# Weaving the block builds of an edge sort between quarters of the next quad's placing steps

## The chip, the cores and the metric

The kernel runs on one core of one Trainium2 chip. The metric is the device time of one execution in microseconds (us), taken without the profiler; the median of several executions is compared. A separate execution is recorded by the hardware profiler, and all rows of traces come from such executions.

## The reference

Four graph layers run on the same graph of 12500 nodes and 412500 edges (each of 200000 random pairs in both directions, and one self loop per node). Between them stand residual additions and layer norms:

```python
edge_index = jnp.stack([src, dst])
x = _layernorm(x + _L0_gnn_ref(x, src, dst, edge_type_8, ...))      # message by edge type, segment_sum over dst, gated update
x = _layernorm(x + _L1_gnn_ref(x, edge_attr_16, We, be, bias, src, dst, 12500))  # 16x16 matrix per edge from its attributes
x = _layernorm(x + _L2_gnn_ref(x, W1, root1, b1, W2, root2, b2, edge_index, edge_type_8))  # two RGCN layers, mean by relation
x = _layernorm(x + _L3_gnn_ref(x, edge_index, W1, b1, W2, b2))      # sheaf layer, messages to src and to dst
```

The edges come sorted by dst. What all layers need is the same: rows of x gathered by src, some arithmetic per edge, and a sum over dst.

## The kernel before, in words

The kernel first sorts the edges once, and the layers after it read the sorted records and selection matrices from HBM. The change lies in this sort stage (`sort_pass`) and in a few lines of the load stage that compute its loop bounds.

**Blocks, quads, steps.** Nodes are cut into 98 blocks of 128 (by dst). Four neighbouring blocks are a quad (Q = 4, QUADS = 25; the last has two real blocks). The edges of a block are read in tiles of 128; a *step* takes five tiles (C = 5) of each of the four blocks of a quad. `quad_steps[n]` is the first step of quad n. The trace below shows 175 steps for 25 quads, so seven per quad, and one step of pads behind them.

**Placing a step.** SyncE loads the attributes of the step's 20 tiles into a ring of eight places (`load_attrs`, L576), ScalarE makes sort keys and copies the fields into the ring (`prepare`, L667, L681), VectorE turns the keys into one-hot matrices (`find`, L825), TensorE counts them (`count`, `count_late`, L730 to L746), VectorE makes from the counts the address of each record (`place`, L847 to L886, the last writes `idx`), and GpSimd issues 20 indirect DMAs that scatter 128 records each into `rec[q]` in HBM (L652). It adds one to the semaphore `scattered` when it reaches the second group of four of a step; the semaphore starts at RING - 1 = 7, so that `scattered >= i + 1`, which VectorE, ScalarE and SyncE wait for, lets them be seven steps ahead of GpSimd and no more.

**Building a block.** When the steps of a quad are scattered, each of its blocks is read back as 128 rows of 40 slots (`load_records`, L584, 420 KB) and VectorE, TensorE and ScalarE make the block's selection matrices (`build` L916 to L944, `turn` with `count_sources` on TensorE, `take_rows` on ScalarE), in one of two halves of `made`. SyncE stores them (`store`, L595 and L596, 3.2 MB). Records of quad n may be read once GpSimd has reached the second group of the first step of quad n + 1: `wait_ge(scattered, i1 + RING)`, where i1 is that step.

**The order** is written out by hand, the same on each engine, and each engine does its own list in order: all steps of quad n + 1, then the four builds of quad n, then the steps of quad n + 2. On VectorE:

```python
one_quad(0)
with dve.Fori(0, QUADS - 1) as n:
    one_quad(n + 1)
    for q in range(Q):
        build(n * Q + q, q & 1)
```

GpSimd has only its 22 turns of eight steps, and no part in the builds. Loop bounds are read from SBUF into registers (`quad_range`, L537 and L538) at each quad.

Of the kernel before, what the change touches and what calls it, by code (L numbers as in the profile page):

```python
# [18 lines left out]
ALU = mybir.AluOpType  # L19
# [21 lines left out]
SPARE = 3  # L41
FIFTH = 3277
# [34 lines left out]
def memory(nc, ctx):  # L77
# [29 lines left out]
    m.quad_tile0 = sb("quad_tile0", [1, QUADS, Q], I32)  # L107
    m.spill = sb("spill", [1, 2 * Q + 1], I32)
# [45 lines left out]
def load_and_constants(nc, m, e, a, tables, rec, spills):  # L154

    with ExitStack() as ctx:
# [23 lines left out]
        limit = sb("limit", [1, QUADS])  # L180
        sofar = [sb(f"sofar{n}", [1, QUADS + 1]) for n in range(2)]
# [16 lines left out]
        with nc.Block() as block:  # L198
# [145 lines left out]
            def _(dve):  # L344
# [69 lines left out]
                link(v.tensor_reduce(sofar[0][:, 1:QUADS + 1], need[:, :, :], AX.X, ALU.max))  # L414
# [7 lines left out]
                link(v.tensor_copy(m.quad_steps[0:1, 0:QUADS + 1], sofar[1][:, :]))  # L422
                link(v.tensor_scalar(odd[:, 1:2], m.quad_steps[0:1, QUADS:QUADS + 1], RING, None, ALU.add))
# [47 lines left out]
def sort_pass(nc, m, e, attr, rec, stream, tail):  # L471

    with ExitStack() as ctx:
# [88 lines left out]
        with nc.Block() as block:  # L562
            @block.sync
            def _(sp):
                rows = attr.rearrange("(t p) f -> p t f", p=P)

                def load_attrs(n):
                    i0, i1 = quad_range(sp, n)
                    t0 = first_tiles(sp, n)
                    with sp.Fori(i0, i1) as i:  # L570
# [27 lines left out]
                def move_blocks(n, blocks):  # L598
# [12 lines left out]
                load_attrs(0)  # L611
                with sp.Fori(0, QUADS - 1) as n:
                    load_attrs(n + 1)
                    move_blocks(n, Q)
# [8 lines left out]
                move_blocks(QUADS - 1, BLOCKS - (QUADS - 1) * Q)  # L623
# [37 lines left out]
            def _(act):  # L661
# [9 lines left out]
                def prepare(n):  # L671
                    i0, i1 = quad_range(act, n)
                    t0 = first_tiles(act, n)
                    act.wait_ge(scattered, i0 + 1)
                    if not isinstance(n, int):
                        act.wait_ge(hot_made, i0 + n)
                    make_keys(n, i0, 0, t0)
                    with act.Fori(i0, i1) as i:
# [5 lines left out]
                        make_keys(n, i + 1, local(i + 1, i0) * C, t0)  # L684

# [25 lines left out]
                prepare(0)  # L711
                with act.Fori(0, QUADS - 1) as n:
# [1749 lines left out]
```

## Time and profile before

| what | value |
|---|---|
| time, median of 3 | 15384.76 us (15326.13 to 15430.24) |
| span of the profiled execution | 18591.9 us |
| sort stage in it (first indirect DMA to the last row of the stage) | 307 to 8506 us |
| GpSimd busy in the sort stage | 3529.38 us in 3520 indirect DMAs |
| VectorE busy in the sort stage | 3770.66 us |

No other time is recorded for the profiled execution than its span, so the span stands for its own time. It is 3207 us longer than the median of the executions without a profiler. The profile's busy times and its order of events can be read as they stand, but its idle times can't all be in the time that is compared.

### The profile page before, as it was taken

The page shows a single profiled execution, that of the slowest core. Times are in us where ns is not written, and L with a number is a line of the kernel's source. Part 1 is how long each engine was busy: PE and PEld are TensorE (multiplying, and loading weights), DVE is VectorE, ACT ScalarE, POOL GpSimd, SP SyncE. Part 2 cuts the span into 40 slices and gives each one's busy share as a digit, 9 for nine tenths or more (in the row PEclk, how much of TensorE's full clock was granted, in tenths as well). Part 3 has the DMA queues.
Part 4 walks back from the last instruction along what each step waited for, and adds up shares of the span by engine and source line. Part 5 has one row for each costly group of instructions (what it writes and reads, how often), then busy time and mean ns, then how long its engine had stood idle before and what let it go on. Part 6 is the DMA issues. An engine that isn't in the chain of part 4 may idle for free. (4 is left out here: it accounts for less than half of the span.)

```text
span 18591.9 us, 463365 instructions
## 1 busy us (share of the span) xinstructions
PE 11767.0 (63%) x159683; PEld 9215.4 (50%) x159684; DVE 12455.0 (67%) x20485; ACT 7662.0 (41%) x16914; POOL 4649.6 (25%) x4771
## 2 busy tenths in 40 slices
PE   1223232232323323236988999979799699999998
PEld 0112122221212212124667888856566588888887
DVE  3345354453544535447887888878788799999998
ACT  1113122221312213124665666656566455555554
POOL 2453434435344343440001111100000111111111
PEclk8555555555555555557999999999999899999999
DMA  7112111111111211115872222268788423333222
GB/s 191 43 40 70 43 61 53 48 62 43 62 51 48 63 42 62 51 55 167 228 208 96 107 108 106 104 176 235 202 235 235 117 84 85 84 85 85 85 84 71
DMA packets 1708077, 1893.34 MB, mean 102 GB/s; under 512 B 979785, under 2 KB 1415579, under 8 KB 1682683
## 3 DMA queue, kind: packets, MB, share of 16 engines
q1 hardware_dynamic: 1588957, 1851.74, 33.4%
q0 software_dynamic: 116864, 39.75, 1.4%
q14 instruction: 148, 1.21, 0.0%
q10 hardware_dynamic: 2078, 0.15, 0.0%
q8 instruction: 30, 0.49, 0.0%
HBM read 1443.55 MB, written 447.40 MB: 102 GB/s over the span
## 5 line engine op out<-in xcount | busy, mean ns | idle before, releaser
L652 POOL DMA_INDIRECT rec<-sort_ring,sort_idx x3520 | 3529.4, 1003 | 4922.3 <-issue 4375.8
L1300 DVE TENSOR_TENSOR e_full<-e_feats,e_masks 128x3840 bf16<-128x3840 bf16 x1179 | 2524.7, 2155 | 343.2 <-ACT e_feats L1258 300.0
L699 ACT CAST sort_rows_dst<-sort_ps_rows 128x512 f16<-128x512 f32 x980 | 532.1, 587 | 5085.7 <-PE sort_ps_rows L768 2659.3
L1213 PE MATMUL e_acc<-e_full,e_sel 128*128 128x384 bf16 (+1 forms) x11760 | 2121.8, 327 | 271.0 <-DVE e_full L1300 270.9
L768 PE MATMUL sort_ps_rows<-ident_h,sort_code 128*128 128x128 f16 x7840 | 1053.3, 300 | 1627.7 <-issue 684.4
L1449 PE MATMUL e_acc<-e_outer,e_sel 128*128 128x272 f32 x7840 | 1897.1, 397 | 5.3 <-DVE e_outer L1544 5.3
L875 DVE TENSOR_TENSOR sort_over<-sort_ps_late,sort_late_base 128x20 f32<-128x20 f32 x175 | 31.1, 178 | 2727.4 <-remote 2090.6
L942 DVE TENSOR_SCALAR sort_made<-sort_rows_code,code_of 128x1664 fp8e4<-128x1664 f16 x882 | 1644.1, 1937 | 192.3 <-ACT sort_rows_code L703 133.8
L730 PE MATMUL sort_ps_count<-sort_hot,upper_b 128*128 x400 | 232.3, 581 | 2422.7 <-DVE sort_hot L825 2219.5
L1256 ACT CAST e_masks<-e_kind 128x1280 bf16<-128x1280 fp8e4 x1179 | 1482.8, 1258 | 624.9 <-DVE e_full L1300 584.0
L768 PEld LDWEIGHTS sort_ps_rows<-ident_h,sort_code 128*128 128x128 f16 x7840 | 663.2, 129 | 2009.0 <-issue 1305.3
L1449 PEld LDWEIGHTS e_acc<-e_outer,e_sel 128*128 128x128 f32 x7840 | 1459.4, 190 | 283.8 <-issue 5.6
L1213 PEld LDWEIGHTS e_acc<-e_full,e_sel 128*128 128x128 fp8e4 x11760 | 1061.2, 97 | 932.9 <-issue 299.5
L730 PEld LDWEIGHTS sort_ps_count<-sort_hot,upper_b 128*128 128x128 bf16 x400 | 49.3, 123 | 2475.5 <-issue 2475.0
L1544 DVE TENSOR_TENSOR e_outer<-e_recb,e_feats 128x2720 f32<-128x2720 f32 x393 | 1173.0, 2985 | 0.0
L1200 PEld LDWEIGHTS e_got<-own,e_hot 128*128 128x128 fp8e4 x34578 | 1037.9, 96 | 194.6 <-issue 78.5
L1200 PE MATMUL e_got<-own,e_hot 128*128 128x48 bf16 x34578 | 1063.9, 183 | 47.5 <-DMA e_hot<-stream 40.7
L2120 PE MATMUL sheaf_ps_v<-w3v,sheaf_hid 128*128 128x32 f32 x7840 | 1052.5, 279 | 0.3 <-ACT sheaf_hid L2024 0.3
L2019 ACT CAST sheaf_xt<-sheaf_ps_xt 102x512 bf16<-102x512 f32 x981 | 575.0, 586 | 1124.5 <-PE sheaf_ps_xt L2093 1107.3
L2144 PE MATMUL sheaf_by_src<-sheaf_msg,sheaf_hot_t 128*128 128x16 bf16 x33939 | 1005.2, 169 | 0.0
L933 DVE TENSOR_SCALAR sort_made<-sort_rows_dst,node 128x4992 fp8e4<-128x4992 f16 x196 | 550.1, 2848 | 676.0 <-ACT sort_rows_dst L699 468.1
L2120 PEld LDWEIGHTS sheaf_ps_v<-w3v,sheaf_hid 128*128 128x128 f32 x7840 | 969.4, 195 | 61.6 <-issue 5.1
(455 smaller groups left out, 25152.8 us busy)
## 6 DMA issues: line engine op xcount, KB each, us to landing
e_hot<-stream SPq DMA_DIRECT2D x888, 480.0 KB, 3.8
stream<-sort_made SPq DMA_DIRECT2D x98, 2568.0 KB, 7.6
e_sel<-stream SPq DMA_DIRECT2D x1176, 160.0 KB, 2.8
e_st<-stream SPq DMA_DIRECT2D x99, 1888.0 KB, 7.3
sheaf_gather<-stream SPq DMA_DIRECT2D x393, 384.0 KB, 3.1
e_hot<-stream SPq DMA_DIRECT2D x294, 448.0 KB, 3.5
tail<-sort_made SPq DMA_DIRECT2D x98, 660.0 KB, 9.3
sheaf_by_dst<-tail SPq DMA_DIRECT2D x491, 128.0 KB, 3.0
```

The source lines that it names most:

```text
L652: nc.gpsimd.indirect_dma_start(out=rec[q], out_offset=bass.IndirectOffsetOnAxis(ap=idx[:, s, q, c:c + 1], axis=0), in_=ring[:, s, q, c, :] ...
L768: last = mm(ps_rows[:, n & 1, k, :], code[:, h, what, j:j + 1].to_broadcast([P, P]), m.ident_h[:, :], start=True, stop=True)
L942: v.tensor_scalar(hot3[:, js, k, :], rows_code[:, js, :], m.code_of[:, k:k + 1], None, ALU.is_equal, saturate=False)
L1200: last = mm(got[q & 1][:, n * 3 * D:(n + 1) * 3 * D], now[:, at * P:(at + 1) * P], rows, start=k == 0, stop=k == spread - 1)
L1213: last = mm(acc[h][:, 0:cols_all], now[:, n * P:(n + 1) * P], full[q & 1][:, n, :], start=j == 0, stop=j == NT - 1)
L1256: nc.scalar.copy(masks[q & 1][:, :, :, :], kinds.unsqueeze(3).to_broadcast([P, BATCH, TYPES, D]))
L1300: v.tensor_tensor(full[q & 1][:, :, 0:cols].rearrange("p j (t k f) -> p j t k f", t=TYPES, k=3), feats[q & 1][:, :, :, :].unsqueeze(2).to_ ...
L1449: last = mm(acc[h][:, 0:cols], sel[q & 1][:, n, :], outer[q & 1][:, n, :], start=j == 0, stop=j == NT - 1)
L1544: v.tensor_tensor(outer[q & 1][:, :, :].rearrange("p j (w f) -> p j w f", f=D), recb[h][:, js, 0:AW].unsqueeze(3).to_broadcast(shape), fea ...
L2019: nc.scalar.copy(xt[k][:, :], ps_xt[0:2 * K3, :]).then_inc(xt_ready, 1)
L2120: last = mm(ps_v[:, at:at + 2 * D], hid[s & 1][:, c * P:(c + 1) * P], m.w3v[:, :], start=False, stop=True, skip_group_check=True)
L2144: last = mm(src_sums((5 * j >> 1) + r), now_t[:, c, r * P:(r + 1) * P], parts[:, p, c, 1, :], start=False, stop=False, skip_group_check=True)
```

## The change

Behind each quarter of a quad's steps each engine now does one block build, one block later than it could at the earliest (LAG = 1). The quarters are made from the quad's number of steps, s: quarter u ends at (s(u+1) + 3) >> 2, which for seven steps is two, two, two and one. The loop of quad n + 1 is: two steps, the last build of quad n - 1, two steps, the first build of quad n, two steps, the second, one step, the third. A quad is given at least four steps. SyncE loads attributes quarter by quarter, and the wait for the quad's scattered records (`landed_all`) moves from behind all seven attribute loads to behind the first two. GpSimd's program is unchanged, as is what a step and a build do.

```diff
+LAG = 1
+UNITS = Q
@@ load stage, VectorE
-                link(v.tensor_reduce(sofar[0][:, 1:QUADS + 1], need[:, :, :], AX.X, ALU.max))
+                link(v.tensor_reduce(per_quad[:, :], need[:, :, :], AX.X, ALU.max))
+                link(v.tensor_scalar(sofar[0][:, 1:QUADS + 1], per_quad[:, :], float(UNITS), None, ALU.max))
...
+                for u in range(UNITS):
+                    link(v.tensor_scalar(units[:, :, u], per_quad[:, :], float(u), float(UNITS - 1), ALU.mult, ALU.add))
+                for u in range(UNITS):
+                    link(v.tensor_scalar(units[:, :, u], units[:, :, u], UNITS.bit_length() - 1, None,
+                                         ALU.arith_shift_right))
+                    link(v.tensor_tensor(units[:, :, u], units[:, :, u], m.quad_steps[0:1, 0:QUADS], ALU.add))
@@ sort stage
+        def unit_range(eng, n, u):
+            return [eng.value_load(m.unit_steps[0:1, bass.ds(n * UNITS + k, 1)], min_val=0, max_val=1 << 20)
+                    for k in (u, u + 1)]
@@ SyncE
-                def move_blocks(n, blocks):
+                def landed_all(n):
                     _, i1 = quad_range(sp, n)
                     sp.wait_ge(scattered, i1 + RING)
                     sp.sem_inc(sp_passed, 1)
-                    load_records(n * Q, n, 0)
-                    load_records(n * Q + 1, n, 1)
-                    for q in range(blocks):
-                        store(n * Q + q, q & 1)
-                        if q + 2 < blocks:
-                            load_records(n * Q + q + 2, n, q + 2)
+
+                def one_quad(n, first):
+                    i0, _ = quad_range(sp, n)
+                    t0 = first_tiles(sp, n)
+                    for u in range(UNITS):
+                        load_attrs(i0, t0, *unit_range(sp, n, u))
+                        b = (n - 1) * Q + u
+                        if not first or u >= LAG + 1:
+                            store(b - LAG - 1, (u - LAG - 1) & 1)
+                        if u == 0:
+                            landed_all(n - 1)
+                        load_records(b, n - 1, u)
@@ ScalarE
+                def one_quad(n, first):
+                    i0, t0 = enter(n)
+                    for u in range(UNITS):
+                        prepare(n, i0, t0, *unit_range(act, n, u))
+                        if not first or u >= LAG:
+                            take_rows((n - 1) * Q + u - LAG, (u - LAG) & 1)
@@ TensorE
+                    for u in range(UNITS):
+                        steps_of(n, *unit_range(pe, n, u))
+                        if not first or u >= LAG:
+                            b = (n - 1) * Q + u - LAG
+                            turn(b, (u - LAG) & 1)
+                            count_sources(b, (u - LAG) & 1)
@@ VectorE
+                def one_quad(n, first):
+                    enter(n)
+                    for u in range(UNITS):
+                        steps_of(n, *unit_range(dve, n, u))
+                        if u == UNITS - 1:
+                            dve.sem_inc(taken, 1)
+                        if not first or u >= LAG:
+                            build((n - 1) * Q + u - LAG, (u - LAG) & 1)
@@ behind the last quad, TensorE, ScalarE and VectorE
-                for b in range((QUADS - 1) * Q, BLOCKS):
+                for b in range((QUADS - 1) * Q - LAG, BLOCKS):
```

Two places in the order of the built programs. On VectorE, in the loop over quads, the end of a build. Before, in the middle of a quad's builds (L944 ends one build, L916 begins the next):

```order
L942 TENSOR_SCALAR sort_made<-sort_rows_code,code_of 128x13x128 x3
L944 TENSOR_SCALAR sort_made<-sort_rows_code,code_of 128x128
L916 ISA
L916 COPY sort_sources<-src_hi 128x15
L917 REGISTER_ALU
L917 COPY sort_sources<-src_lo 128x15
```

The changed kernel between the end of a step's placing (L933 is the old L886), a build (L964 is the old L916) and the next quarter's loop (L557 is `unit_range`):

```order
L933 TENSOR_TENSOR sort_idx<-sort_whole,sort_over 128x20
...
L964 COPY sort_sources<-src_hi 128x15
...
L557 TENSOR_LOAD unit_steps
...
L557 TENSOR_LOAD unit_steps
...
L947 UNCONDITIONAL_BRANCH
```

So a build is now followed by two register loads from SBUF and a jump into the next loop of steps, four times per quad.

On SyncE, in the loop over quads, from the attribute loads of a step to the read of the records (L600 belongs to the wait for the scattered records). Before, the loop over seven steps ends, and both records and stores follow:

```order
L576 DMA sort_ring<-in_attr 128x5x16
L570 REGISTER_ALU
L570 COMPARE_AND_BRANCH
...
L600 REGISTER_ALU
...
L584 DMA sort_recb<-rec 128x840
...
L584 DMA sort_recb<-rec 128x840
```

The changed kernel after the first quarter, which is two steps (L612 and L613 are the store, L617 the wait, L601 the read, L593 an attribute load of the next quarter):

```order
L593 DMA sort_ring<-in_attr 128x5x16
L587 REGISTER_ALU
L587 COMPARE_AND_BRANCH
...
L612 DMA stream<-sort_made 128x10272
...
L613 DMA tail<-sort_made 128x2640
...
L617 REGISTER_ALU
...
L601 DMA sort_recb<-rec 128x840
```

The store of an earlier block now stands ahead of the wait, and the attribute loads of five of the seven steps stand behind it.

## Rows read from the trace of the kernel before

**Rows 1.** The page: span, busy times, and 40 slices of the span.

```profile
span 18591.9 us, 463365 instructions
...
PE 11767.0 (63%) x159683; PEld 9215.4 (50%) x159684; DVE 12455.0 (67%) x20485; ACT 7662.0 (41%) x16914; POOL 4649.6 (25%) x4771
...
DVE  3345354453544535447887888878788799999998
...
POOL 2453434435344343440001111100000111111111
```

**Rows 2.** Windows of the span: before the sort, the sort, behind it.

```profile
core 0: us, PE busy (x) PEld busy (x) DVE busy (x) ACT busy (x) POOL busy (x), PEclk, DMA share, GB/s
0.00:307.00 307.00, 32.44 (x170) 20.15 (x171) 131.82 (x216) 68.56 (x175) 2.88 (x20) 1.00 1.04 281
307.00:8506.00 8199.00, 2468.81 (x22352) 1719.66 (x22352) 3770.66 (x5350) 1900.21 (x4397) 3529.38 (x3520) 0.52 0.18 53
8506.00:18592.00 10086.00, 9265.73 (x137161) 7475.63 (x137161) 8552.47 (x14919) 5693.22 (x12342) 1117.34 (x1231) 0.96 0.47 136
```

**Rows 3.** One line, GpSimd's indirect DMAs: count, duration ns min/median/max, waits.

```profile
L652 POOL DMA_INDIRECT rec<-sort_ring,sort_idx x3520: 962/967/2396, 307.6 to 8454.5; - x196
...
  issue: 4375.8, 3420
  DVE sort_idx L886: 541.6, 84
  DMA rec<-sort_ring,sort_idx: 4.9, 16
```

**Rows 4.** Timeline of GpSimd, start of the sort's first two steps.

```profile
start us, us, engine line op out<-in xcount [idle before <-releaser]
307.55 1.67 POOL L652 DMA_INDIRECT rec<-sort_ring,sort_idx  x1 [303.84 <-issue]
309.53 1.00 POOL L652 DMA_INDIRECT rec<-sort_ring,sort_idx  x1 [0.30 <-issue]
...
332.44 0.97 POOL L652 DMA_INDIRECT rec<-sort_ring,sort_idx  x1 [0.30 <-issue]
338.89 1.70 POOL L652 DMA_INDIRECT rec<-sort_ring,sort_idx  x1 [5.48 <-DVE sort_idx L886]
```

**Rows 5.** Timeline of GpSimd around the builds of one quad, and its last quad's.

```profile
2038.85 0.97 POOL L652 DMA_INDIRECT rec<-sort_ring,sort_idx  x1 [0.31 <-issue]
2170.03 0.97 POOL L652 DMA_INDIRECT rec<-sort_ring,sort_idx  x1 [130.22 <-issue]
...
8109.44 0.97 POOL L652 DMA_INDIRECT rec<-sort_ring,sort_idx  x1 [129.90 <-issue]
...
8454.46 0.97 POOL L652 DMA_INDIRECT rec<-sort_ring,sort_idx  x1 [0.30 <-issue]
```

**Rows 6.** Timeline of VectorE, turn to the next quad, its first step, the second.

```profile
2154.51 0.28 DVE L944 TENSOR_SCALAR sort_made<-sort_rows_code,code_of 128x128 fp8e4<-128x128 f16 x1
2157.49 0.19 DVE L893 MEMSET sort_base<- 128x160 f32 x1 [2.71 <-issue]
...
2162.84 1.06 DVE L847 TENSOR_TENSOR sort_before<-sort_ps_count,sort_base 128x400 f32<-128x400 f32 x2 [2.58 <-PE sort_ps_count L736]
...
2169.98 1.05 DVE L847 TENSOR_TENSOR sort_before<-sort_ps_count,sort_base 128x400 f32<-128x400 f32 x2
...
2198.77 0.18 DVE L875 TENSOR_TENSOR sort_over<-sort_ps_late,sort_late_base 128x20 f32<-128x20 f32 x1 [24.28 <-remote]
```

**Rows 7.** Two lines of VectorE: the wait in each step, the turn of each quad.

```profile
L875 DVE TENSOR_TENSOR sort_over<-sort_ps_late,sort_late_base x175: 169/179/180, 305.2 to 8276.8; 128x20 f32<-128x20 f32 x175
...
  remote: 2090.6, 116
...
L893 DVE MEMSET sort_base<- x25: 192/192/192, 293.0 to 8096.8; 128x160 f32 x25
...
  issue: 66.2, 25
```

**Rows 8.** Timeline of VectorE, the first build of a quad and the next two starts.

```profile
2350.24 0.17 DVE L916 COPY sort_sources<-src_hi 128x15 bf16 x1 [0.24 <-issue]
...
2350.86 3.76 DVE L909 TENSOR_TENSOR own<-sort_sources,iota 128x1470 fp8e4<-128x1470 bf16 x2
...
2363.56 11.20 DVE L942 TENSOR_SCALAR sort_made<-sort_rows_code,code_of 128x1664 fp8e4<-128x1664 f16 x6
...
2387.50 0.18 DVE L916 COPY sort_sources<-src_hi 128x15 bf16 x1 [0.25 <-issue]
...
2417.52 0.17 DVE L916 COPY sort_sources<-src_hi 128x15 bf16 x1 [0.24 <-issue]
```

**Rows 9.** Timeline of GpSimd beside that first build.

```profile
2351.01 2.38 POOL L652 DMA_INDIRECT rec<-sort_ring,sort_idx  x1 [7.24 <-DVE sort_idx L886]
2353.69 1.76 POOL L652 DMA_INDIRECT rec<-sort_ring,sort_idx  x1 [0.30 <-issue]
2355.76 0.96 POOL L652 DMA_INDIRECT rec<-sort_ring,sort_idx  x1 [0.30 <-issue]
...
2364.65 0.96 POOL L652 DMA_INDIRECT rec<-sort_ring,sort_idx  x1 [0.30 <-issue]
...
2377.36 0.97 POOL L652 DMA_INDIRECT rec<-sort_ring,sort_idx  x1 [0.30 <-issue]
```

**Rows 10.** DMA issues by line, KB each, median us to landing.

```profile
stream<-sort_made SPq DMA_DIRECT2D x98, 2568.0 KB, 7.6
...
e_recb<-rec SPq DMA_DIRECT2D x99, 420.0 KB, 7.9
```

**Rows 11.** Timeline of SyncE's queue, the attribute loads of seven steps.

```profile
2164.98 65.78 SPq L576 DMA_DIRECT2D sort_ring<-in_attr  x28
```

More of the change, by code:

```diff
@@ L41 @@
 SPARE = 3
+LAG = 1
+UNITS = Q
+assert UNITS == 4
 FIFTH = 3277
@@ L622, in _ @@
                         sp.dma_start(ring[:, place_of(i), q, :, 0:D].squeeze(1), rows[:, 0:C, :]).then_inc(attr_in, 16)
-                move_blocks(QUADS - 1, BLOCKS - (QUADS - 1) * Q)
+                for b in range((QUADS - 1) * Q, BLOCKS):
+                    store(b - LAG - 1, (b - LAG - 1) & 1)
+                    if b == (QUADS - 1) * Q:
+                        landed_all(QUADS - 1)
+                    load_records(b, QUADS - 1, b % Q)
+                for b in range(BLOCKS - LAG - 1, BLOCKS):
+                    store(b, b & 1)
                 sp.wait_ge(spill_made, 1)
@@ L783, in _ @@
                 pe.sem_inc(ends_summed, 2)
-                one_quad(0)
-                with pe.Fori(0, QUADS - 1) as n:
-                    one_quad(n + 1)
-                    for q in range(Q):
-                        turn(n * Q + q, q & 1)
-                        count_sources(n * Q + q, q & 1)
-                for b in range((QUADS - 1) * Q, BLOCKS):
+                i0, i1 = quad_range(pe, 0)
+                count(i0)
+                steps_of(0, i0, i1)
+                one_quad(1, True)
+                with pe.Fori(1, QUADS - 1) as n:
+                    one_quad(n + 1, False)
+                for b in range((QUADS - 1) * Q - LAG, BLOCKS):
                     turn(b, b & 1)
@@ L897, in one_quad, with steps_of @@
                     find(i0, n)
-                    with dve.Fori(i0, i1) as i:
+                def steps_of(n, start, end):
+                    with dve.Fori(start, end) as i:
                         find(i + 1, n)
                         place(i, n)
-                    dve.sem_inc(taken, 1)
                 def split_sources(b, h):
@@ L948, in build, with one_quad @@
                     dve.sem_inc(built, 1)
-                one_quad(0)
-                with dve.Fori(0, QUADS - 1) as n:
-                    one_quad(n + 1)
-                    for q in range(Q):
-                        build(n * Q + q, q & 1)
+                def one_quad(n, first):
+                    enter(n)
[5 more added lines that the diff above has]
+                            build((n - 1) * Q + u - LAG, (u - LAG) & 1)
+                enter(0)
+                steps_of(0, *quad_range(dve, 0))
+                dve.sem_inc(taken, 1)
+                one_quad(1, True)
+                with dve.Fori(1, QUADS - 1) as n:
+                    one_quad(n + 1, False)
                 i0, i1 = all_steps(dve)
@@ L959, in _ @@
                         .then_inc(idx_ready, 1)
-                for b in range((QUADS - 1) * Q, BLOCKS):
+                for b in range((QUADS - 1) * Q - LAG, BLOCKS):
                     build(b, b & 1)
```

51 lines of the change are left out of this document (28 added, 23 removed).

## The prediction

> **What bounds the kernel now.** I read the page first, for the stages: the sort takes the slices in which GpSimd is busy, some 45% of the span, and no engine is over 50% busy there [rows 1]. The windows give its edges: 8199 of 18592 us, GpSimd busy 3529, VectorE 3771; behind it VectorE and TensorE are at 85% and more, and the change touches nothing [rows 2]. The whole question is the sort.
>
> There the indirect DMAs set the pace that can't be beaten. The timeline of GpSimd shows starts 1.27 us apart (0.97 busy, 0.30 between), twenty to a step, so 25.4 us a step [rows 4], and 3520 of them [rows 3], 176 steps: 4470 us. The other 3600 us of the stage GpSimd is idle in the profiled execution (8199 - 3529 - 3520 x 0.30 = 3614), most plainly once a quad: 130 us between two steps, while four builds run [rows 5]. Seven steps of 25.4 us, six waits of some 5.5 us for the next addresses [rows 4] and one of 130 us make 341, near the 8199 / 25 = 328 us of a mean quad.
>
> Read so, the weaving should give back a good part of 24 x 130 us. But the next view speaks against it. VectorE could be seven steps ahead, and it isn't: it waits in the middle of a step for a count by TensorE, 24 us in one case, until GpSimd has issued its twenty DMAs [rows 6], and that wait takes 2090.6 us in 116 steps, put down to nobody's instruction [rows 7]. A step whose counts come at once takes VectorE 7.14 us from one L847 to the next [rows 6]. Something holds the other engines while GpSimd issues in the profiled execution. And that execution is 18591.9 - 15384.8 = 3207 us longer than the median. Behind the sort there is little room for such a loss: the engines are as good as full [rows 2]. So I put all of it in the sort, where the idle time is. That is my choice, and the forecast rests on it: without the profiler the sort takes 8199 - 3207 = **4992 us**, of which GpSimd issues for at least 4470.
>
> **GpSimd's path.** Beside VectorE's instructions with two operands in SBUF an indirect DMA takes longer. The first of a step takes 1.67 or 1.70 us [rows 4], 0.7 more than the others, for 175 steps 122 us. Beside L909 of a build two took 2.38 and 1.76 [rows 9], 2.2 more together; for 98 builds at most 216 us. The rest of the same build, L933 and L942, left them at 0.96 and 0.97 [rows 8, 9]. Sum: 4470 + 122 + 216 = 4808, and 51 from the last issue at 8455.4 to 8506 [rows 2, 5]: **4859 us**, with no gap at all. The median leaves 4992 - 4859 = **133 us** of idle time for the whole sort. For one quad of seven steps GpSimd needs 7 x 26.1 + 4 x 2.2 = **191.5 us**.
>
> The Trainium skill (SBUF — State Buffer, section Who interferes with whom) says that tensor_scalar and cast can hold a port pair that GpSimd needs, and that tensor_tensor doesn't stop descriptor generation. Rows 8 and 9 show the reverse here. By that rule L933 and L942 (5.6 and 16.8 us) would stop GpSimd for 22.4 us a build, 2195 us in all, and the sort could not be under 6665 us; the median has no room for that, and the rows decide.
>
> **VectorE's path.** The turn to the next quad, from the end of L944 (2154.79) to L847 (2162.84), 8.05 us; seven steps of 7.14, 50.0; four builds of 30.0 (2387.50 to 2417.52), 120.1 [rows 6, 8]: **178.1 us** a quad, 13 under GpSimd. Does the old order let GpSimd run dry? Take as zero the moment when GpSimd reaches the second group of a quad's first step and the records of the quad before may be read. 6.75 placed steps lie ahead of it, 185 us with the two-operand stops. VectorE needs the read (7.9 us by the nearest row of 420 KB [rows 10]), 120 us of builds, the turn and one step: 143 us. It is 42 us early. So the seven places of the ring already cover the builds, and the weaving has **nothing to fill: 0 us**.
>
> **The changed order, part by part.** Steps, builds, DMAs and bytes are the same in number; 25 quads of seven steps are over the new minimum of four. Removed: nothing. Moved: at the zero of above VectorE has placed four steps instead of seven, so GpSimd has 3.75 steps, 98 us, ahead of it; VectorE owes it the read, one build, the loads of a bound and one step, 7.9 + 30 + 2.7 + 7.1 = 48 us. It is 50 us early: no loss. On SyncE the wait for the records now stands ahead of five of seven attribute loads, and a store of 3.2 MB may be queued ahead of them. Seven steps of loads took 65.8 us with their waits, so one at most 9.4 [rows 11]; with the record read (7.9) and a store (7.6 to 9.3; [rows 10] has the larger part) and a landing, taken like the read, it is 34 us. The third step is needed at 46 us. Hidden, with 12 us left; were this cover gone, GpSimd would wait for what lies beyond 46 us, once a quad.
>
> Added: on each of four engines, at each quarter, two register loads and an entry of a loop. No row shows that pair alone; the nearest is the turn of a quad on VectorE, 66.2 / 25 = 2.65 us for a back branch and two loads [rows 7], and the other end is nothing. I take the row: 4 x 2.65 = 10.6 us, and VectorE's quad becomes **188.7 us**, still 2.8 under GpSimd's. ScalarE, TensorE and SyncE pay the same and have more room: none is busier than TensorE's 2469 of 8199 [rows 2]. On the load stage some ten more VectorE instructions on 25 numbers stand in a chain. The nearest row is a VectorE instruction on 20 columns, 0.18 us [rows 7]; with as much again between two it is 4 us. At the end both orders leave the last two builds behind the last step. Sum: 0 + 4, **15389 us**. A GpSimd bound stays one, and VectorE loses most of its slack.
>
> **Rivals.** *The idle time is real and the weaving fills it.* For it: rows 5, and rows 8: a build beside a step of GpSimd took 37.3 us instead of 30.0, so 25.4 us of GpSimd were covered for 7.3. Three more such builds in 24 quads give 3 x 18.1 x 24 = 1300 us in the profiled execution, where 3614 are idle. Without the profiler only what is idle there can come back: 133 us if all of the 3207 lies in the sort. If 500 us of it lie elsewhere (the clock of TensorE is granted at 0.96 behind the sort, so not there; a longer load stage, or slower issues by GpSimd under the profiler, would do it), 633 are idle, and 1300 / 3614 of them is 228. So 15385 - 133 to - 228: about 15200 us. With the excess spread evenly, 1300 x 15385 / 18592 = 1076 us, 14300; against that stands that nothing behind the sort shows a wait like rows 7. Chance of the rival 0.24, of the large form 0.05 in it.
>
> *VectorE becomes the bound, slower.* The place is the quad loop, the price the 10.6 us of loads, less the room. It decides from 191.5 - 188.7 = 2.8 us a quad more on VectorE, or as much less on GpSimd. For it: a mean quad without the profiler is (4992 - 51) / 25 = 197.7 us, 6 more than GpSimd's path, and builds beside GpSimd need not take 30.0 (37.3 in rows 8; four of those would make 207, more than the median allows). If VectorE's path is the 197.7, nearly all of 24 x 10.6 = 254 us is added: 15385 + 254 = 15640; with a part of it, 15540. Against it: loads in a row of which a half is the branch. Chance 0.18.
> The Trainium skill (Runtime: NRT & Kernel Launch, section Instruction fetch mechanics) gives some 0.2 us for a register load and warns of a fetch stall at a taken branch outside of two pages; by its loads alone the price is 8 x 0.2 x 24 = 38 us, and no row here splits the 2.65 us.
>
> *The wait moves to SyncE.* The 12 us of cover above are gone when a store delays the attributes; 10 us a quad would be 240. It ends at the same time as the second rival and shares its chance.
>
> **How the numbers follow.** Chances: forecast 0.58, its own range 15250 to 15520; faster 0.24; slower 0.18. One per cent, 154 us, is about what a measurement of this kernel can tell from no change (the three runs span 104 us). The range reaches down to the modest form of the first rival and up to the full price of the second, **15140 to 15650**, and leaves out the large form and the tails of both, 0.15 or so.
>
> **What the profile after would show.** Right: GpSimd has no gap of 130 us any more, each build lies beside part of a step, the span of the profiled execution falls by several hundred us, up to 1300, and the median doesn't move: the profiled span and the median come apart. GpSimd's DMAs stay 1.27 us apart. The loads at a quarter cost 1 to 3 us on VectorE. The first rival is right if the median falls with the span; the second if the median rises while VectorE's gaps at the quarters are over 3 us each, or its builds beside GpSimd over 32. The forecast fails at its root if the 3207 us don't lie in the sort.

## The result, and the profile after

The changed kernel takes **15445.77 us** (median of 7 runs, 15402.72 to 15482.38), the kernel before, run beside it, 15370.91 us (7 runs, 15326.13 to 15430.24): a ratio of **1.0047 [1.0027, 1.0067]**. That is within one per cent, as forecast, but clear of 1, and 57 us above the predicted 15389. But the profiled execution of the changed kernel spans 15401.0 us where that of before spanned 18591.9 [rows 1], over 3000 us less, and the forecast had been several hundred, up to 1300.

The page of the changed kernel: span, and the 40 slices of GpSimd.

```profile
span 15401.0 us, 466034 instructions
...
POOL 1777777777777500011111100000001111111111
```

The sort now takes some 13 slices instead of 18 [rows 1], and GpSimd is at 70% and more in the twelve that lie wholly in it. This looks like the weaving at its best. It isn't: the unchanged kernel, profiled again in two of the experiments below, gave both pictures. Here is its page where its time is 15336 us (run again2):

```profile
span 15333.7 us, 463365 instructions
...
POOL 1777777777777400011111100000001111111111
```

**One fact is needed to read everything that follows: the chips used are of two kinds for this kernel.** On one (the chip of the result, and chip 2) the kernel before takes 15331 to 15371 us; on the other (chips 14 and 11) it takes 18613 to 18668 us, in every run, with the profiler or without it. They are called the fast and the slow chip here. By its span the profile before (18591.9 us) came from a slow chip, and the times beside it came from a fast one. Each set of experiments ran on one chip and is compared with the kernel before on that chip; whether it is the chip itself that differs, or something that held while a set ran, these runs don't separate.

The windows of the sort and of what follows it: the changed kernel on the fast chip; the kernel before on the fast chip; the kernel before on the slow chip. The columns are those of rows 2.

```profile
307.00:5328.00 5021.00, 2415.34 (x22352) 1705.37 (x22352) 3738.36 (x5350) 1888.30 (x4401) 3639.95 (x3520) 0.52 0.31 87
5328.00:15401.00 10073.00, 9251.30 (x137161) 7463.67 (x137161) 8552.46 (x14919) 5692.89 (x12342) 1113.06 (x1231) 0.96 0.47 136
```

```profile
307.00:5250.00 4943.00, 2398.84 (x22352) 1699.65 (x22352) 3737.80 (x5350) 1881.66 (x4399) 3676.20 (x3520) 0.54 0.30 88
5250.00:15334.00 10084.00, 9263.40 (x137161) 7480.70 (x137161) 8549.60 (x14919) 5693.75 (x12342) 1116.16 (x1231) 0.96 0.47 136
```

```profile
307.00:8505.00 8198.00, 2473.44 (x22352) 1723.30 (x22352) 3765.00 (x5351) 1899.85 (x4397) 3515.13 (x3520) 0.53 0.18 53
```

Behind the sort the stage is the same (10073, 10084, and 10086 in rows 2). The sort of the kernel before is 8198 us on the slow chip and 4943 on the fast one. The change makes it 5021: **78 us longer**. (These two profiles are of two fast chips, that of the result and chip 2. The changed kernel's own profile on chip 2 is read below.) The busy times don't tell why, since GpSimd's even falls by 36 us (3676.20 to 3639.95; 307 of its DMAs take over 1.2 us instead of 330). What GpSimd waited for does. The indirect DMAs' line, of the changed kernel and then of the kernel before, both on the fast chip (engine, operation, count, ns; then idle us and how often, by what ended it):

```profile
L681 POOL DMA_INDIRECT rec<-sort_ring,sort_idx x3520: 962/967/2957, 307.0 to 5277.7; - x196
...
  issue: 1105.2, 3346
  ACT sort_ring L713: 303.3, 1
  DMA rec<-sort_ring,sort_idx: 222.3, 159
  DMA sort_ring<-in_attr: 4.3, 14
```

```profile
L652 POOL DMA_INDIRECT rec<-sort_ring,sort_idx x3520: 962/969/2449, 307.9 to 5198.6; - x196
...
  issue: 1405.8, 3374
  DMA rec<-sort_ring,sort_idx: 108.7, 129
  DMA sort_ring<-in_attr: 4.3, 14
```

The one long wait for the load stage (some 303 us) is in "issue" before and a row of its own after, so the issue gaps are the same, 1102 and 1105 us. No address is waited for (no row for sort_idx), before or after. Attributes cost 4.3 us in both. What doubled is GpSimd's wait for its own DMAs to land, **108.7 to 222.3 us**: +113.6, less the 36.3 of busy time, is 77, against 80 by which the line's first start to its last end grew (4891.7 to 4971.7). The changed kernel profiled on chip 2 itself (run woven, 15410.9 us) shows the same at a smaller size. Its row:

```profile
  DMA rec<-sort_ring,sort_idx: 211.4, 154
```

That is +102.7, less 36.1 of busy time, 67, against 64 (4891.7 to 4955.3). Of the 77 us between the two profiled spans on this chip (15410.9 and 15333.7) some 62 lie in the sort. So two profiles of one kernel differ by 11 to 16 us here, and the terms below are no finer than that.

Where are these waits? SyncE's queue of the changed kernel on the fast chip, and GpSimd a few us later:

```profile
2086.61 0.37 SPq L612 DMA_DIRECT2D stream<-sort_made  x1
2087.16 0.36 SPq L613 DMA_DIRECT2D tail<-sort_made  x1
...
2092.04 12.27 SPq L593 DMA_DIRECT2D sort_ring<-in_attr  x8
```

```profile
2094.77 0.97 POOL L681 DMA_INDIRECT rec<-sort_ring,sort_idx  x1 [0.30 <-issue]
2099.44 0.97 POOL L681 DMA_INDIRECT rec<-sort_ring,sort_idx  x1 [3.70 <-DMA rec<-sort_ring,sort_idx]
```

A block's store (2.6 + 0.66 MB) is issued at 2086.6, and 12.8 us later GpSimd, which starts a group of four DMAs only when the group before the last has landed, waits 3.70 us. This holds throughout: of the changed kernel's waits of this kind, 86 are over 0.8 us (200.1 us together), and **after all 86 GpSimd's DMA starts 7.1 to 14.0 us behind a store's issue**. Of the kernel before it is all 62 (88.3 us together, 7.0 to 12.7 us behind a store), and of the changed kernel on chip 2 all 89 (191.1 us, 8.8 to 14.7). By chance it would be one in five: 167 and 187 of the 880 group starts lie 4 to 16 us behind a store. So the waits belong to the stores by their place. The change has more of them and longer ones, 2.3 us instead of 1.4. Some 90 of the 98 stores lie beside GpSimd's issues: 62 waits follow before, 86 and 89 after. A second DMA lies beside many stores, the read of a block's records 1.3 us behind. It is there at 42 of the 90 stores before and at 64 in woven, and the landing waits behind these are longer (1.28 and 2.25 us a store in the mean, against 0.72 and 1.90 behind the others). A part of the weaving's share may be the read's.

### The profile page after: what moved, and what is told of

Read it like the earlier page. It is cut to its first block and busy times, and to the rows that moved or that the text cites. A ratio compares the mean times of both kernels' runs of the same rounds, so it can differ in the third digit from the quotient of the medians.

```text
span 15401.0 us, 466034 instructions
## 1 busy us (share of the span) xinstructions
PE 11698.7 (76%) x159683; PEld 9188.8 (60%) x159684; DVE 12425.3 (81%) x20500; ACT 7649.1 (50%) x16914; POOL 4755.9 (31%) x4771
## 5 line engine op out<-in xcount | busy, mean ns | idle before, releaser
L681 POOL DMA_INDIRECT rec<-sort_ring,sort_idx x3520 | 3640.0, 1034 | 1635.0 <-issue 1105.2
L2202 PEld LDWEIGHTS sheaf_by_src<-sheaf_msg,sheaf_hot_t 128*128 128x128 bf16 x33939 | 969.5, 96 | 2.9 <-issue 2.9
L2082 ACT ACTIVATE sheaf_hid<-sheaf_ps_h,b 128x512 f32<-128x512 f32 x981 | 674.2, 687 | 513.4 <-PE sheaf_ps_h L2160 511.7
```

The lines of the kernel that those rows point to most:

```text
L681: nc.gpsimd.indirect_dma_start(out=rec[q], out_offset=bass.IndirectOffsetOnAxis(ap=idx[:, s, q, c:c + 1], axis=0), in_=ring[:, s, q, c, :] ...
L2082: nc.scalar.activation(hid[k][:, :], ps_h[:, :], ACT.Relu, bias=m.b1[:, 0:1]).then_inc(hid_ready, 1)
L2202: last = mm(src_sums((5 * j >> 1) + r), now_t[:, c, r * P:(r + 1) * P], parts[:, p, c, 1, :], start=False, stop=False, skip_group_check=True)
```

## The experiments

Three sets, each on one chip. The medians, and the ratio to the kernel before on that chip, with its 95% interval (it is not the ratio of the medians, and differs from it by up to 0.001). The kernel before takes 18620.6 us on chip 14, 15331.6 on chip 2 and 18667.7 on chip 11:

| kernel | chip | us | ratio |
|---|---|---|---|
| before, again (again) | 14, slow | 18613.1 | 0.999 [0.9975, 1.0005] |
| split_only | 14, slow | 18663.1 | 1.0023 [1.0009, 1.0036] |
| after_land4 | 14, slow | 18184.0 | 0.9767 [0.9741, 0.9792] |
| before_land4 | 14, slow | 18490.4 | 0.993 [0.9911, 0.9949] |
| before, again (again2) | 2, fast | 15336.3 | 1.0002 [0.999, 1.0015] |
| the changed kernel (woven) | 2, fast | 15426.4 | 1.0053 [1.0036, 1.0071] |
| split_only2 | 2, fast | 15361.2 | 1.001 [0.9999, 1.0021] |
| woven_loads | 2, fast | 15699.9 | 1.0235 [1.0211, 1.0258] |
| the changed kernel (woven2) | 11, slow | 18254.3 | 0.9779 [0.9753, 0.9806] |
| after_land4b | 11, slow | 18305.7 | 0.9809 [0.9787, 0.9832] |
| before_land4b | 11, slow | 18610.3 | 0.9978 [0.9961, 0.9995] |
| store_twice | 11, slow | 18809.1 | 1.0088 [1.0059, 1.0117] |

### First set (chip 14)

**The kernel before, once more**, without an edit.

> The kernel before, unchanged, timed against itself. Its time should be that of before (ratio 1.000 within 0.2%), which shows what the measurement can tell. Its profile decides between two readings of the 3207 us by which the profiled execution of before was longer than the median: if the order of steps and builds makes the profiler hold the engines, the new profile has a span of some 18600 us again and a gap of 130 us on GpSimd at each quad; if it was that one execution, the span is within 100 us of 15370 and GpSimd issues without gaps. The profile after had a span of 15401 us with seven steps of the first quad in a row, as before, so I expect the second.

It took 18613.1 us in the median of its timed runs, and 18651.2 profiled. The expectation was wrong: its span is long again, and so are its times. The profiler isn't what makes it long. So the choice on which the forecast rests (3207 us of profiler in the sort) fell with this run. The count by TensorE on which VectorE waits in each step is here as in rows 7 (line of VectorE, and what ended its idle time):

```profile
L875 DVE TENSOR_TENSOR sort_over<-sort_ps_late,sort_late_base x175: 170/179/180, 305.0 to 8272.5; 128x20 f32<-128x20 f32 x175
its engine sat idle before it (us, times) until:
  remote: 2631.7, 143
```

**The split loops in the old order.** The loops of the changed kernel, with its bounds, its register loads and its four loops a quad, but the builds behind the whole quad again. One engine's part of the edit; SyncE, ScalarE and TensorE have the like:

```diff
-                        if u == UNITS - 1:
-                            dve.sem_inc(taken, 1)
-                        if not first or u >= LAG:
-                            build((n - 1) * Q + u - LAG, (u - LAG) & 1)
+                    dve.sem_inc(taken, 1)
+                    for q in range(Q):
+                        build((n - 1) * Q + q, q & 1)
```

> The kernel before, with each quad's steps cut into the four loops of the change on every engine (register loads and loop entries added), but with all four builds behind them and SyncE's loads, waits and stores in the old order. Theory 'register loads': the added loads and loop entries are what costs the 75 us, so this kernel takes some 15445 us too (ratio 1.005). Theory 'collisions on GpSimd's path': the loads hide behind GpSimd, ratio 1.000 within 0.002, and the 75 us come from where the builds, stores and attribute loads now fall. In its profile VectorE still waits for records once a quad under the second theory.

18663.1, +0.23% on this chip. The gaps of a quad are as before (24, of 126.4 us in the mean against 126.8 in again); the trace puts them to another releaser, a row of its L679:

```profile
  DMA sort_ring<-in_attr: 2672.8, 22
```

The 22 waits "for attributes" are 121 us each. Attributes aren't what was late: the queue that loads them stands behind the records' wait in the old order too, and the old kernel shows the same gaps with the releaser "issue" [rows 5]. It is the name of whatever came last by the profile.

**Four semaphores instead of two** for the landing of GpSimd's DMAs, so that a group waits for the fourth before it instead of the second; in the changed kernel and in the kernel before. The edit has two more parts: GpSimd adds to `scattered` at the fourth group of a step instead of the second, so that ring places come free and records may be read two groups later, and the spare rows (`trash`, `none`) get five places instead of three. The line for the wait:

```diff
-                            pool.wait_ge(landed[at & 1], u * (16 * Q * C // 2) + (at >> 1) * (16 * Q))
+                            pool.wait_ge(landed[at & 3], u * (16 * Q * C // 4) + (at >> 2) * (16 * Q))
```

> The changed kernel, with four semaphores for the landing of GpSimd's scatters in place of two, so that a group of four waits for the group four before it and not two before it (trash rows get five places in place of three, and the place is given free at the fourth group of a step). In the profile after GpSimd waited 222 us for its own scatters to land, 159 times. Theory 'GpSimd bound': those waits go and the time falls by 100 to 220 us, to about 15230 to 15340. Theory 'VectorE bound': nothing falls, 15445 within 20 us.

> The kernel before with the same four landing semaphores. If the 75 us that the change costs are landing waits (stores and attribute loads now lying beside more of the scatters), this kernel gains less than the changed one does, and the two come out equal, within 0.2%. If the 75 us are something else, both gain the same and stay 75 us apart. With GpSimd as the bound the gain is 50 to 220 us, with VectorE none.

Ratios 0.9767 and 0.993. The kernel before gained 130 us from it, though GpSimd hardly waits for landings on this chip (7.0 us in 23, in the run of the kernel before). The repeat on chip 11 gave 57 us. The traces show where it came from: GpSimd's 24 long gaps are 117.4 us in the mean instead of 126.8, and VectorE's first build of a quad, part of which lies beside GpSimd's issues, takes 35.7 us instead of 58.4 (the third and fourth take 30.2 in both). So it is the build, and not the landing wait, that got shorter. Which part of the edit does it was not tried; the later `scattered`, which lets the builds start later, is one that could. On its own the first ratio couldn't say whether the weaving or the semaphores made the gain, and the third set had to.

### Second set (chip 2)

> The changed kernel, unchanged, beside the kernel before on one chip. The last four runs were on a chip on which the kernel before takes 18620 us, not 15371, and in all its runs, not only when profiled. So the forecast's root ('the 3207 us are the profiler's') is wrong: there are two kinds of chip for this kernel. If this is the slow kind, GpSimd has 3500 us of gaps there and each build should cover a part of a step: I expect the ratio at 0.965 to 0.985 (with four landing semaphores the changed order was 306 us faster than the old). If it is the fast kind: ratio 1.003 to 1.006, as first measured.

> The kernel before, unchanged, for a profile on this chip. On a chip of the fast kind it should have no gap of 130 us on GpSimd, GpSimd's landing waits and stops should sum to some 75 us less than the 222 + 239 us of the changed kernel's profile if collisions are the cost, and the same if the loads are. On the slow kind it is a second profile like the first.

> Steps cut into four loops on every engine, builds and SyncE's order as before. On the slow chip it cost 42 us (1.0023). Theory 'register loads': the cost of the change on the fast kind is this part, ratio 1.004 to 1.006. Theory 'collisions': 1.000 within 0.002 on the fast kind. On a slow chip again 1.002.

**woven_loads** is the changed kernel with three more pairs of register loads at each quarter, on VectorE alone:

```diff
+                        for _ in range(3):
+                            unit_range(dve, n, u)
```

> The changed kernel with three more pairs of the register loads at each quarter, on VectorE alone; their values aren't used. Twelve pairs a quad of 0.6 us each without a branch (two TENSOR_LOAD of 0.3) up to 1.9 us make 7 to 23 us on VectorE's path of a quad. If GpSimd is the bound (fast kind), VectorE waits 15 us a quad for records in the profile after and takes it out of that: under 40 us more than the changed kernel. If VectorE is the bound: 170 to 550 us more.

This chip is a fast one, and its runs settle most. The changed kernel is 95 us above the kernel before by the medians (1.0053), which repeats the result. **The world of the forecast exists**: the kernel before has a sort of 4943 us, where 4992 was put, and VectorE's line that waited 2631.7 us on the slow chip has no row of idle time at all:

```profile
L875 DVE TENSOR_TENSOR sort_over<-sort_ps_late,sort_late_base x175: 164/171/179, 305.6 to 4989.4; 128x20 f32<-128x20 f32 x175
its engine sat idle before it (us, times) until:
who waited for it (us, times):
```

Instead VectorE waits for keys, a ring place that GpSimd hasn't freed, 506.3 us in 41 waits. VectorE of the kernel before, its first line of a step; then the same line of the changed kernel; then of woven_loads:

```profile
  ACT sort_keys L667: 506.3, 41
  issue: 79.9, 111
```

```profile
  issue: 239.5, 153
```

```profile
  issue: 889.5, 171
```

The change's loads and loop entries cost VectorE up to 239.5 - 79.9 = 160 us there, and 135.0 instead of 66.0 at the turn of a quad:

```profile
L940 DVE MEMSET sort_base<- x25: 192/192/192, 292.6 to 4981.6; 128x160 f32 x25
...
  issue: 135.0, 25
```

```profile
L893 DVE MEMSET sort_base<- x25: 192/192/192, 293.3 to 4917.3; 128x160 f32 x25
...
  issue: 66.0, 25
```

That is 229 us, or 9.5 a quad over 24 quads, of the forecast 10.6. It is an upper end: 153 gaps against 111 are counted, and an ordinary one of 0.7 us that stood under the wait for keys before is in "issue" now. The 76 gaps over 2 us alone (179.3 us, less 0.72 each) and the turn make 194 us, 8 a quad. Do they cost time? The split alone has them all, and took 1.001 [0.9999, 1.0021], some 30 us by the medians; the interval holds 1. Twelve more pairs a quad cost VectorE 650 us (889.5 - 239.5), 2.3 us a pair where 0.6 to 1.9 was expected. These pairs are dearer than the change's own, as the rows of the loads on VectorE's queue show, of the changed kernel and of woven_loads:

```profile
L557 DVEq TENSOR_LOAD <-unit_steps x192: 298/308/929, 351.6 to 5141.8; - x192
```

```profile
L557 DVEq TENSOR_LOAD <-unit_steps x768: 297/890/1052, 351.8 to 5457.8; - x192
```

Of the eight loads in a row in woven_loads the first two take 0.31 us each in the median, like the two of the changed kernel, and from the third on 0.80 to 0.92. The kernel took 273 us more than the changed kernel beside it. The other 377 were hidden, 377 / 24 = 15.7 us a quad. A part of this is the lead of several steps that VectorE has at the start and loses once: GpSimd first waits long for addresses at 1279 us, and from 1491 to 5306 us once a quad, 211.9 us apart. Less the 650 / 24 = 27.1 of the added loads, VectorE's quad in the changed kernel is some 184.8 us. The changed kernel's own pace is 198.9 us a quad (690 to 5065 us, 22 quads). So the **room is some 14 us a quad** in the woven order. Beyond it VectorE is the bound, and GpSimd's waits name it (woven_loads, the indirect DMAs' line):

```profile
  DVE sort_idx L933: 310.9, 22
...
  DMA rec<-sort_ring,sort_idx: 173.0, 157
```

The same room can be read without an experiment from VectorE's waits in the changed kernel. Its 25 waits for a quad's records sum to 371.3 us, but the first (73.0, the start) and the last (41.4, the end) are of another kind; the 23 between are 11.2 us each. With 3.0 us a quad for a count by TensorE (72.6 us in 18 waits) that is 14 again:

```profile
L967 DVE CAST sort_code<-sort_recb x98: 185/201/278, 495.6 to 5285.1; 128x40 f16<-128x40 f32 x98
...
  DMA sort_recb<-rec: 371.3, 25
```

And split_only2 splits the landing waits. Its row:

```profile
  DMA rec<-sort_ring,sort_idx: 179.0, 155
```

So of the landing waits **70.3 us come with the split loops in the old order**, in which the stores haven't moved, and 32 with the weaving (211.4 against 179.0, both on chip 2; 43 by the profile of the other fast chip). Its 85 waits over 0.8 us all lie 7.0 to 14.2 us behind a store too. GpSimd's busy time is 45.6 us lower at once (3630.6 against 3676.2), so that only 22 us of GpSimd's path, and 30 of the kernel's time, are left. The biggest difference by place is at the third store of a quad: a wait follows it in 3 of 24 quads before and in 20 of 24 in split_only2.

What else comes with the split is code. The DMA queues in the window of the sort, packets, MB and share of 16 engines: the changed kernel, then the kernel before, both fast chip.

```profile
q8 instruction: 235, 3.85, 0.3%
q14 instruction: 260, 2.13, 0.2%
```

```profile
q14 instruction: 124, 1.02, 0.1%
q8 instruction: 8, 0.13, 0.0%
```

495 packets of code instead of 132, in split_only2 452. They don't account for the waits of the kernel before by their place: 96 of 248 stretches of 20 us have such a packet, and 23 of its 62 landing waits over 0.8 us have one in the 20 us ahead of them, no more than chance. Of its 90 stores beside GpSimd's issues a wait follows 57 of the 64 without a packet near (from 5 us ahead to 14 behind), and only 5 of the 26 with one, most of these being a quad's third store. In the changed kernel the same test can tell nothing, as 224 of its 252 stretches have one. An experiment on code beside a store was not made.

### Third set (chip 11)

> The changed kernel with four landing semaphores (a group of scatters waits for the one four before it). On a fast chip (kernel before at 15331 us) the changed kernel's GpSimd waited 211 us for landings against 109 in the kernel before, and all of the excess gaps lie 5 to 15 us behind a store of 3.2 MB. Theory 'landings behind stores': the waits go (the part over a bare issue is 164 us), ratio to before 0.994 to 0.998, and the changed kernel stands where before_land4b stands within 25 us. Theory 'something else costs the 80 us': it stays 60 to 100 us behind before_land4b. On a slow chip as before, ratio 0.977.

> The kernel before with four landing semaphores. On a fast chip its excess gaps behind stores are 70 us in all; if they go, the ratio is 0.995 to 0.997 (15255 to 15290 us). If VectorE sets the pace, 1.000. On a slow chip 0.993 again.

**store_twice** is the kernel before with a third DMA behind each block's store, which writes its 2568 KB part once more, to a tensor that nothing reads:

```diff
+                    sp.dma_start(twice[bass.ds(b, 1), :, :].squeeze(0), made[:, h, 0:ST_CODE // 2]).then_inc(stored, 16)
```

> The kernel before, in which each block's 2.6 MB are stored a second time, to a place that nothing reads. Theory 'landings behind stores': the stores take nearly twice as long, the excess gaps of 70 us grow to 150 us or more, and the time rises by as much, ratio 1.004 to 1.015 on a fast chip. If stores have nothing to do with the gaps, the time stays within 20 us.

> The changed kernel, unchanged. On a slow chip (kernel before at 18620 us), where it hasn't been timed, ratio 0.97 to 0.985, since four landing semaphores made the changed order 306 us faster than the old one there. On a fast chip 1.005 again, and beside after_land4b it gives what the landings cost.

The chip is a slow one, and there these couldn't test what they were made for. With 1.8 times the bytes in each block's stores the landing waits are 6.4 us in 21 (7.0 in 23 without), the sort is 8371 us instead of 8198, and the kernel 141 us longer. The added time is in the 24 long gaps, 133.3 us each instead of 126.8, and not in landing waits. **That the stores cause the landing waits on the fast chip is thus read from where the waits lie, and not shown by an experiment.** Four semaphores beside the same weaving are no gain: 18305.7 against 18254.3. So the first set's 0.9767 was the weaving's.

What the set does show is the weaving on a slow chip: woven2 is **0.9779 [0.9753, 0.9806], 413 us faster** than the kernel before. Its window of the sort, and the indirect DMAs' line:

```profile
307.00:8132.00 7825.00, 2472.31 (x22352) 1708.03 (x22352) 3748.68 (x5350) 1938.33 (x4401) 3643.23 (x3520) 0.52 0.19 56
```

```profile
  DVE sort_idx L933: 3007.8, 135
  issue: 1079.4, 3345
...
  DMA rec<-sort_ring,sort_idx: 11.0, 36
```

The 24 long gaps are gone, and in their place stand 135 waits for addresses, 22 us each. GpSimd's gap and VectorE's build beside it, of woven2:

```profile
2033.14 0.96 POOL L681 DMA_INDIRECT rec<-sort_ring,sort_idx  x1 [0.30 <-issue]
2071.72 1.57 POOL L681 DMA_INDIRECT rec<-sort_ring,sort_idx  x1 [37.62 <-DVE sort_idx L933]
```

```profile
2006.03 0.17 DVE L964 COPY sort_sources<-src_hi 128x15 bf16 x1 [0.24 <-issue]
...
2030.98 5.65 DVE L990 TENSOR_SCALAR sort_made<-sort_rows_code,code_of 128x1664 fp8e4<-128x1664 f16 x3 [5.83 <-ACT sort_rows_code L742]
...
2044.87 0.28 DVE L992 TENSOR_SCALAR sort_made<-sort_rows_code,code_of 128x128 fp8e4<-128x128 f16 x1
```

This build takes 39.1 us (2006.03 to 2045.15) where it took 30.0 alone: VectorE waits 5.83 us for rows from ScalarE while GpSimd issues. It is one of the shorter ones. The 98 builds of woven2 take 38.3 us in the median and 44.4 in the mean, the longest 68.7. And when GpSimd has used up its addresses the step that makes the next ones has yet to be placed. VectorE's own wait in the steps fell from 2631.7 us in 143 (chip 14) to the row below.

```profile
  remote: 1397.4, 78
```

So a build beside GpSimd's issues does take the place of waiting, and 373 us of the sort come back (8198 to 7825; the first is of chip 14, where the kernel before is 47 us faster than on chip 11), not the 1300 that three covered steps a quad would have given.

## Why the prediction was right, and where it was not

**The time: right, by luck in one term.** 15446 lies in the forecast's own range (15250 to 15520), the ratio within one per cent. 57 us are missing from the total. The change itself was put at +4 us and measured +75 beside the kernel before; 14 us of the difference are hidden by the older median from which the sum starts (15385, and 15371 with more runs).

**"The 3207 us are the profiler's, all in the sort": half wrong.** All of it does lie in the sort (8198 against 4943, 3255 us). But it is the kind of chip, not the profiler. The forecast compared a profile from one kind of chip with times from the other, and the sentence "without the profiler the sort takes 4992 us" should have read "on the chip of the times". The number is 49 us off. The step survived only because the subtraction gives the same result whatever the cause. On chips of the kind that the profile came from, the forecast of no change is wrong: there it is 2.2% faster.

**GpSimd's path, 4859 us with no gap: right.** The line runs 4892 us on the fast chip with 108.7 us of landing waits, so 4783 without them, where the sum had 4808 ahead of the 51 at the end. The 133 us of idle time left over were real and were mostly landing waits, which rows 3 show as 4.9 us only. On the slow chip every profile has few of them (at most 11.0 us).

**"The weaving has nothing to fill, 0 us": right on the fast chip**, where the kernel before waits for no address, and VectorE waits 506 us for GpSimd.

**The missing term: the landing waits.** The part on what is moved counted a store ahead of attribute loads, and found them hidden. They are (4.3 us before and after). It didn't ask whether the indirect DMAs in flight beside a store land later. That term measured +103 to +114 us, less 36 us of GpSimd's busy time. Of this 70 came with the split and 32 to 43 with the weaving. No cause of the first part is shown: the split moves no store, and what it does change is the loops, their loads, and 320 more packets of code in the sort (363 in the changed kernel). That stays open.

**The register loads, 10.6 us a quad for VectorE: right** (8 to 9.5), and hidden as said. **"2.8 us under GpSimd": too little.** The room is some 14 us a quad. GpSimd's quad is 197.7 us by the forecast's own mean (198.9 by its pace after) and not 191.5; the difference had been left out of the room because it couldn't be put to an engine. And VectorE's is some 185 us and not 188.7. With 14 us of room VectorE's rival would have deserved less than 0.18. The 38 us by the Trainium skill's figure (Runtime: NRT & Kernel Launch, section Instruction fetch mechanics) would be a sixth to a fifth of the 194 to 229 measured. A load alone takes 0.31 us in the median, and such a row was in the trace of before too (L537 on VectorE's queue, 307 ns), though the forecast says that none splits the 2.65 us. From the start of the first load of a quarter to the end of the second it is 1.06 us; the rest is the bounds' register work and the loop's entry.

**The wait moves to SyncE: false**, by the attributes' row.

**The first rival: true on the slow chip, at a third of its size**, 373 us in the sort for 1300. Its price took a build beside a step at 37.3 us from one build, and let GpSimd run on. The median of woven2 is near it (38.3), but the mean is 44.4. The same trace could have warned: the first builds of its 24 quads, part of which lie beside GpSimd's issues, take 54.0 us in the mean, and that of rows 8 is among the shorter ones. And GpSimd stops when its 20 addresses are used, as the build is longer than a step of 25.4 us.

**The signs in the profile.** No gap of 130 us: right, for the wrong reason, since the kernel before has none on that chip either. The profiled span falls and the median doesn't: as forecast in form, but the fall of 3191 us is the chip's. The forecast named its own point of failure, the place of the 3207 us. It would have been better to name their cause, which one more run of the unchanged kernel tells.

## What to carry to other kernels

When a profiled span and the times beside it are far apart, settle first whether they are from the same chip: run the unchanged kernel in the same set, and argue from the profile that belongs to the times. Filling an idle engine pays only where it idles in the world that is timed; here the same edit is worth -2.2% on one kind of chip and +0.5% on the other. Where large stores lie beside small DMAs whose landing is waited for, the landing waits are a term of the sum (109 us before, 211 to 222 after). Splitting a loop can move other waits even when every instruction that it adds is hidden: 70 us of landing waits came with the split, though 46 us of GpSimd's busy time went and the kernel's time hardly moved. When one instruction's length is taken for a price, look at all of its kind: the one build in the forecast took 37 us, and the mean of those beside GpSimd was 54. None of the kernels that were timed on both kinds of chip (the changed one and the split) is faster on both.

## What the runs showed of the hardware

- **Two kinds of chip.** The same program, 15331 us on one chip and 18613 to 18668 on two others, with all of the difference in the stage in which GpSimd issues 3520 indirect DMAs. GpSimd's own pace is the same (median 967 to 969 ns, 0.30 between). On the slow kind other engines stand idle while it issues (VectorE's count wait: 2631.7 us in 143 against none). TensorE too: its small matmuls L745 and L746 have 491.3 and 445.6 us of "issue" gaps before them in the sort of again (240 and 215, up to 3.3 us each), and none in again2. What differs in the chips stays open, and so does whether it stays with a chip.
- **A landing wait 7 to 15 us behind a 3.2 MB store.** All of 62, 85, 86 and 89 waits over 0.8 us in four profiles of three kernels lie there (7.0 to 14.7 us); they are 1.4 to 2.3 us in the mean. Only by their place, as said.
- **Register loads in a row get dearer.** The first two of a row on VectorE take 0.31 us each in the median, with 1.06 us from the start of the first to the end of the second (after). In a row of eight (woven_loads) the third takes 0.80 and the others 0.91 to 0.92, so that 288 pairs more cost 650 us, 2.3 us each. Why is open.
- **More loops, more code by DMA:** 495 packets in the sort instead of 132, 6.0 MB instead of 1.1.
